# A decoder layer on one core: the key bias added by VectorE instead of a matmul, the normalisation of later groups on ScalarE

## The chip, the cores and the metric

The kernel runs on one core of a Trainium2 chip. The metric is the device time of one execution in microseconds. TensorE multiplies matrices, VectorE and ScalarE do elementwise work, GpSimd (POOL) does small side work, SyncE (SP) starts most transfers. Every engine takes its own instructions strictly in order and waits for the others by semaphores.

## The reference: what is computed

One pre-norm decoder layer over x of 2 x 2048 rows of 512 numbers, in float32. `ln` is a layer norm without weights. Only the first part matters here:

```
xn = ln(x)
k = xn @ Wk + bk ;  q = xn @ Wq + bq ;  v = xn @ Wv + bv
K = elu(k) + 1 ;    Q = elu(q) + 1                       # 8 heads of 64
KV = sum over rows of K v^T ; x1 = x + (Q KV) / (Q . sum of K)
x2 = x1 + cross attention of ln(x1) with a context of 77 rows
out = x2 + mixture of 8 experts, top 2, on ln(x2)
```

## The kernel before

The rows are worked on in 8 groups of 512 (4 tiles of 128 rows). Stage one goes over all groups and makes the keys' feature map, the queries' for the first four groups, and the Gram matrix xn^T K from which KV follows. Stage two goes over the groups again (attention, cross attention, routing), stage three over the experts. The change touches stage one alone.

Float32 accuracy comes from splitting each operand into a high and a low part (`_hi` by ScalarE, `_lo` = value - high by VectorE), and each product is three matmuls of 512 columns (`three`, lines 915 to 919). So a group s (0 to 7) of stage one is, engine by engine:

- TensorE: `project(s)`: four key tiles j = 0 to 3, each a bias product (L1023: a matrix of ones times the bias) and 12 products, into PSUM bank `pj[j % 2]`; in groups 0 to 3 four query tiles of 12 products (L917 to L919) more, into the same two banks. Then `gram(s)`, four tiles of 12 products into `pg`, and between them `turn(s + 1)`, 16 transposes (L935) of the next group's `xn` in two halves. The first half wants `xn`, the second also `xT_lo` of the first (s_tlo). In group 1 the cross attention's products (L951 to L975) stand between the query tiles, in group 2 L983 and L992.
- ScalarE: `turned_hi` (L688), `xn_hi` (L718, waits for the Gram products of the group before), then for each tile exp and relu of the bank (L695, L696: `job`), and for keys `k_hi` (L700).
- VectorE: `turned_lo`, `xn_lo` (both L1333), `next_stats(s + 1)` (L1337, L1343: mean and variance of the next input), then for each tile `kf` or `qT` from exp and relu (L1371: `job`), `k_lo` (L1333), and in the middle `normalise(s + 1)` (L1350: `xn`).
- POOL: the reciprocal of the standard deviation (L499, L500: `rstd_in`) and the sum of the keys (L548).

TensorE has two banks, so tile j waits until bank j - 2 has been read: `s_feat`, which ScalarE raises behind its relu. The order within an engine is written by hand.

Of the kernel before, what the change touches and what calls it, by code (L numbers as in the profile page):

```python
# [13 lines left out]
F32R = mybir.dt.float32r  # L14
# [21 lines left out]
BR = 33  # L36
# [42 lines left out]
def decoder(nc, x, wq, wk, wv, bq, bk, bv, ctxT, xwqT, xbq, xwk, xbk, xwv4, xbv4, wout, bout,  # L79
# [181 lines left out]
    with ExitStack() as ctx:  # L261
# [16 lines left out]
        s_bk = sem("bk_rows_cleared")  # L278
# [91 lines left out]
        XATTN_LOADS, WOUT_LOADS, WK_LOADS, WQ_LOADS, WV_LOADS = 7, 5, 3, 2, 2  # L370
# [118 lines left out]
        def _(pool):  # L489
# [180 lines left out]
        def _(act):  # L670
# [19 lines left out]
            def job(s, j):  # L690
                act.wait_ge(s_proj, FIRST[s] + j + 1)
                if s or j >= 2:
                    act.wait_ge(s_fm, FIRST[s] + j - 1)
                bias = 0.0 if j < TI else bq_c[:, j - TI:j - TI + 1]
                a.activation(fe[j % 2][:], pj[j % 2][:], ACT.Exp, bias=bias)  # L695
                a.activation(frl[j % 2][:], pj[j % 2][:], ACT.Relu, bias=bias).then_inc(s_feat, 1)  # L696
# [14 lines left out]
            for s in range(GROUPS):  # L711
# [202 lines left out]
        def _(pe):  # L914
# [855 lines left out]
```

## Time and profile before

| | |
|---|---|
| median of 3 runs | 1554.58 us (1553.37 to 1557.08) |
| the profiled execution | 1555.67 us, its span 1554.0 us |
| mean granted TensorE clock | 0.969 |
| TensorE busy | 1447.5 us (93%) |
| VectorE, ScalarE, POOL busy | 626.7, 569.1, 358.3 us |
| stage one | 0 to 292.2 us |

The span is from the first to the last instruction; the time of the execution has 1.67 us more around it. Busy time is the time in which an engine had an instruction in hand. DVE, ACT, POOL, PE stand for VectorE, ScalarE, GpSimd, TensorE; PEld is the load of a matmul's weights.

### The profile page before, as it was taken

Reading aid. Unit: us, or ns where it says so; the run is one execution under the profiler, and the core shown is the slowest. Engines: PE = TensorE matmul, PEld = TensorE weight load, DVE = VectorE, ACT = ScalarE, POOL = GpSimd, SP = SyncE. Lnnn points to the kernel's source line nnn. Section 1 sums busy time; section 2 is a strip of 40 time slices with the busy share of each in tenths; the row PEclk is TensorE's granted clock in tenths of the full one; section 3 lists DMA queues with packets and bytes.
Section 4 is the critical chain, followed back from the end, with each engine's and each line's share of the span. In section 5 each row is a group of like instructions: output and inputs, shape, how many; then the busy total and the mean of one; then the engine's idle time right before and its main releaser. Section 6 shows DMA issues by size and latency. Waiting matters only on the chain.

```text
span 1554.0 us, 20925 instructions
## 1 busy us (share of the span) xinstructions
PE 1447.5 (93%) x7326; PEld 1215.5 (78%) x7327; DVE 626.7 (40%) x1383; ACT 569.1 (37%) x977; POOL 358.3 (23%) x346
## 2 busy tenths in 40 slices
PE   6999999999984499999999899999999999999998
PEld 4867877787872387888888788898789888897886
DVE  5634565467876143411342531215431431215211
ACT  4433433257865133312342522224432432214211
POOL 3201232137665302011112112021112112021111
PEclk9999999999996599999999999999999999999999
DMA  9200221229546416121353332035533342035112
GB/s 197 52 4 28 82 82 54 82 79 210 129 124 196 135 56 163 55 40 14 64 178 54 120 99 40 0 54 176 155 88 54 103 114 40 0 54 149 13 40 27
DMA packets 78985, 132.19 MB, mean 85 GB/s; under 512 B 30388, under 2 KB 30516, under 8 KB 77912
## 3 DMA queue, kind: packets, MB, share of 16 engines
q1 hardware_dynamic: 62520, 97.40, 22.0%
q0 software_dynamic: 16416, 34.16, 11.8%
q8 instruction: 28, 0.46, 0.1%
q14 instruction: 21, 0.17, 0.0%
HBM read 93.63 MB, written 37.91 MB: 85 GB/s over the span
## 4 chain that ended last, share of the span: by engine, by line
PE 81%; DVE 5%; POOL 4%; DMA 4%; issue 3%; ACT 2%; SPq 0%; ACTq 0%; DVEq 0%; POOLq 0%
PE pg L917 16%; PE pg L918 15%; PE pg L919 15%; PE pj L917 8%; PE pj L919 8%; PE pj L918 8%; POOL slot_table L589 2%; DMA slot_table<-pack,dest 2%; PE pt L1270 1%; PE pg L1176 1%; PE pj L1148 1%; DVE w_lo L1333 1%; DMA stage<-w 1%; PE pg L1114 1%; PE pt L935 1%
## 5 line engine op out<-in xcount | busy, mean ns | idle before, releaser
L917 PE MATMUL pg<-xe_hi,w_hi 128*128 128x512 f32 (+2 forms) x1088 | 394.0, 362 | 22.2 <-DVE w_lo L1333 12.8
L918 PE MATMUL pg<-xe_lo,w_hi 128*128 128x512 f32 (+2 forms) x1088 | 393.0, 361 | 0.0
L919 PE MATMUL pg<-xe_hi,w_lo 128*128 128x512 f32 (+2 forms) x1088 | 392.7, 361 | 0.0
L1705 DVE TENSOR_TENSOR hp<-gl,pg 128x512 f32<-128x512 f32 (+1 forms) x136 | 87.1, 641 | 606.7 <-ACT gl L870 606.7
L650 POOL DMA_INDIRECT out_rows<-ost,etab x62 | 99.2, 1600 | 801.2 <-ACT ost L897 402.5
L917 PEld LDWEIGHTS pg<-xe_hi,w_hi 128*128 128x128 f32 x1088 | 207.6, 191 | 53.9 <-DVE w_lo L1333 14.8
L870 ACT ACTIVATE gl<-pg 128x512 f32<-128x512 f32 (+1 forms) x136 | 76.1, 560 | 456.6 <-PE pg L919 456.6
L919 PEld LDWEIGHTS pg<-xe_hi,w_lo 128*128 128x128 f32 x1088 | 207.7, 191 | 28.4
L918 PEld LDWEIGHTS pg<-xe_lo,w_hi 128*128 128x128 f32 x1088 | 207.7, 191 | 28.2
L917 PE MATMUL pj<-w_hi,hg_hi 128*128 128x512 f32 x464 | 183.3, 395 | 0.0
L919 PE MATMUL pj<-w_hi,hg_lo 128*128 128x512 f32 x464 | 180.8, 390 | 0.0
L918 PE MATMUL pj<-w_lo,hg_hi 128*128 128x512 f32 x464 | 180.7, 390 | 0.0
L1333 DVE TENSOR_TENSOR w_lo<-stage,w_hi 128x1024 fp32r<-128x1024 f32 x96 | 115.0, 1223 | 33.5 <-ACT w_hi L810 32.8
L897 ACT ACTIVATE ost<-pj,etab 128x512 f32<-128x512 f32 x62 | 42.6, 688 | 200.6 <-PE pj L919 194.3
L810 ACT ACTIVATE w_hi<-stage 128x1024 fp32r<-128x1024 f32 x96 | 99.0, 1057 | 40.3 <-DMA stage<-w 39.3
L919 PEld LDWEIGHTS pj<-w_hi,hg_lo 128*128 128x128 f32 x464 | 87.1, 188 | 18.3
L918 PEld LDWEIGHTS pj<-w_lo,hg_hi 128*128 128x128 f32 x464 | 87.2, 188 | 17.2
L917 PEld LDWEIGHTS pj<-w_hi,hg_hi 128*128 128x128 f32 x464 | 87.2, 188 | 17.1
L1333 DVE TENSOR_TENSOR hg_lo<-hp,hg_hi 128x512 fp32r<-128x512 f32 (+1 forms) x136 | 87.0, 639 | 1.9
L873 ACT ACTIVATE hg_hi<-hp 128x512 fp32r<-128x512 f32 (+1 forms) x136 | 79.8, 587 | 4.1 <-DVE hp L1705 4.1
L589 POOL DMA_INDIRECT slot_table<-pack,dest x64 | 67.5, 1055 | 23.1 <-issue 17.2
L1333 DVE TENSOR_TENSOR xe_lo<-pt,xe_hi 128x512 fp32r<-128x512 f32 x66 | 42.6, 685 | 71.3 <-ACT xe_hi L850 71.1
(233 smaller groups left out, 1946.3 us busy)
## 6 DMA issues: line engine op xcount, KB each, us to landing
stage<-w SPq DMA_DIRECT2D x96, 512.0 KB, 4.9
xr<-x SPq DMA_DIRECT2D x8, 1024.0 KB, 9.4
out_rows<-xr SPq DMA_DIRECT2D x8, 1024.0 KB, 7.2
x_rows<-xn SPq DMA_DIRECT2D x8, 1024.0 KB
x_in<-x SPq DMA_DIRECT2D x7, 1024.0 KB, 5.5
late_xT<-xT_hi SPq DMA_DIRECT2D x2, 1024.0 KB, 3.9
late_xT<-xT_lo SPq DMA_DIRECT2D x2, 1024.0 KB, 6.0
xT_hi<-late_xT SPq DMA_DIRECT2D x2, 1024.0 KB, 4.7
```

The costliest lines, as they stand in the source:

```text
L589: p.indirect_dma_start(out=table, out_offset=bass.IndirectOffsetOnAxis(ap=dest[:, c:c + 1], axis=0), in_=pack[:, c, :], in_offset=None).th ...
L650: p.indirect_dma_start(out=out, out_offset=bass.IndirectOffsetOnAxis(ap=etab[:, t, 0:1], axis=0), in_=ost[i % 2][:], in_offset=None, compu ...
L810: a.activation(w_dst(s), stage[s % STG][:], ACT.Copy).then_inc(s_w_hi, 1)
L870: a.activation(gl[j % 2][:, 0:w], pg[:, j % 2, 0:w], ACT.Gelu).then_inc(s_gl, 1)
L873: a.activation(hg_hi[:, j - 1, 0:w], hp[(j - 1) % 2][:, 0:w], ACT.Copy).then_inc(s_hghi, 1)
L897: a.activation(ost[i % 2][:], pj[i % 2][:], ACT.Copy, scale=etab[:, t, 1:2].bitcast(F32)).then_inc(s_yev, 1)
L917: nc.tensor.matmul(o, lh, rh, start=start, stop=False)
L918: nc.tensor.matmul(o, lh, rl, start=False, stop=False)
L919: return nc.tensor.matmul(o, ll, rh, start=False, stop=stop)
L935: ins = nc.tensor.transpose(pt[k % 2][:, i * P:(i + 1) * P], xn[:, i, k * P:(k + 1) * P], ident[:])
L1333: return v.tensor_tensor(dst, src, hi.bitcast(F32), ALU.subtract)
L1705: v.tensor_tensor(hp[j % 2][:, 0:w], gl[j % 2][:, 0:w], pg[:, 2 + j % 2, 0:w], ALU.mult).then_inc(s_hp, 1)
```

## The change

The bias product of each key tile goes (32 products), with the ones, the bias parts and their making. Instead the bias is loaded into all 128 partitions (`bk_all`), and VectorE adds it to each key tile out of PSUM into a tile `kb[j % 2]` (`key_bias`); ScalarE's exp and relu then read `kb`. The bank is free for TensorE when the addition is done (`s_kb`). VectorE's order in a tile becomes: bias of tile j, `k_lo` of tile j - 1, `kf` of tile j. ScalarE makes `k_hi` of tile j - 1 ahead of exp and relu of tile j, no longer behind. The normalisation of groups 1 to 7 goes from VectorE to ScalarE, as x * rstd + shift, at the same place of the loop; POOL makes the shift with two small instructions more.

```diff
@@ SyncE
-            for dst, src in ((wk_raw[:], wk.rearrange("(k p) n -> p k n", p=P)),
-                             (bk_rows[0:1, :], bk), (bk_rows[BR - 1:BR, :], bk)):
-                sp.dma_start(dst, src).then_inc(s_wk_in, 16)
+            sp.dma_start(wk_raw[:], wk.rearrange("(k p) n -> p k n", p=P)).then_inc(s_wk_in, 16)
+            sp.dma_start(bk_all[:], bk.broadcast_to([P, D])).then_inc(s_bk, 16)
@@ GpSimd, rstd_in
-                inverse_std(0).then_inc(s_rstd, 1)
+                if s == 0:
+                    inverse_std(0).then_inc(s_rstd, 1)
+                    return
+                pool.wait_ge(s_xn, s)
+                p.tensor_scalar(neg_mean[0][:], mv[0][:, :, 0], -1.0, None, ALU.mult)
+                step(inverse_std(0))
+                p.tensor_tensor(shift[0][:], neg_mean[0][:], rstd[0][:], ALU.mult).then_inc(s_rstd, 1)
@@ ScalarE
-            a.activation(ones_r[:], ones[:], ACT.Copy).then_inc(s_yev, 1)
-            a.activation(bk_parts[:], zrow[:], ACT.Copy).then_inc(s_bk, 1)
             act.wait_ge(s_wk_in, 16 * WK_LOADS)
             a.activation(wk_hi[:], wk_raw[:], ACT.Copy).then_inc(s_whi, 1)
-            act.wait_ge(s_bk, 1)
-            a.activation(bk_parts[0:1, :], bk_rows[0:1, :], ACT.Copy)
-            a.activation(bk_parts[BR - 1:BR, :], bk_rows[BR - 1:BR, :], ACT.Copy).then_inc(s_whi, 1)
...
+            def normalise(s):
+                act.wait_ge(s_rstd, s + 1)
+                act.wait_ge(s_xnhi, s)
+                act.wait_ge(s_xnlo, s)
+                for i in range(TI):
+                    ins = a.activation(xn[:, i, :], x_in[:, i, :], ACT.Identity, bias=shift[0][:, i:i + 1],
+                                       scale=rstd[0][:, i:i + 1])
+                ins.then_inc(s_xn, 1)
@@ ScalarE, loop over a group's tiles
+                    if 1 <= j <= TI:
+                        khi(s, j - 1)
                     if j < JOBS[s]:
                         job(s, j)
-                    if 1 <= j <= TI:
-                        khi(s, j - 1)
+                    if s + 1 < GROUPS and j == (TI if s == 0 else 2):
+                        normalise(s + 1)
@@ TensorE, project
-                    if s or j >= 2:
-                        pe.wait_ge(s_feat, FIRST[s] + j - 1)
+                    if j >= 2 or s:
+                        b, c = (s, j - 2) if j >= 2 else (s - 1, JOBS[s - 1] + j - 2)
+                        if c < TI:
+                            pe.wait_ge(s_kb, b * TI + c + 1)
+                        else:
+                            pe.wait_ge(s_feat, FIRST[b] + c + 1)
...
-                        mm(o, ones_r[:], bk_parts[:], start=True, stop=False)
@@ VectorE
+            def key_bias(s, j):
+                dve.wait_ge(s_proj, FIRST[s] + j + 1)
+                if s or j >= 2:
+                    b, c = (s, j - 2) if j >= 2 else (s - 1, TI + j - 2)
+                    dve.wait_ge(s_feat, FIRST[b] + c + 1)
+                v.tensor_tensor(kb[j % 2][:], pj[j % 2][:], bk_all[:], ALU.add).then_inc(s_kb, 1)
@@ VectorE, loop over a group's tiles
-                    if j < JOBS[s]:
-                        job(s, j)
+                    if j < TI:
+                        key_bias(s, j)
                     if 1 <= j <= TI:
                         ...
+                    if j < JOBS[s]:
+                        job(s, j)
                     if s == 0 and j == 2:
                         next_stats(1)
-                    if s + 1 < GROUPS and j == (TI if s == 0 else 2):
-                        normalise(s + 1)
```

The first place is VectorE at the start of group 1 (it reads alike in groups 2 to 6), from `xn_lo` on. In the kernel before, with `exp_relu_ready` for s_feat and `proj_psum_ready` for a finished bank:

```order
L1333 TENSOR_TENSOR xn_lo<-xn,xn_hi 128x2048 [waits xn_hi_ready]
L1337 BN_STATS st_71<-x_in 128x6 [waits x_in_loaded]
L1337 BN_STATS st_71<-x_in 128x6 x3
L1343 BN_AGGR mv_73<-st_71 128x2 [waits dve_step]
L1343 BN_AGGR mv_73<-st_71 128x2 x3
L1371 SCALAR_TENSOR_TENSOR kf_142<-fe_138,frl_140 128x512 [waits k_lo_ready,k_sum_added,exp_relu_ready]
L1371 SCALAR_TENSOR_TENSOR kf_143<-fe_139,frl_141 128x512 [waits k_lo_ready,k_sum_added,exp_relu_ready]
L1333 TENSOR_TENSOR k_lo<-kf_142,k_hi 128x512 [waits feature_map_ready,k_hi_ready]
L1371 SCALAR_TENSOR_TENSOR kf_142<-fe_138,frl_140 128x512 [waits k_lo_ready,k_sum_added,exp_relu_ready]
L1333 TENSOR_TENSOR k_lo<-kf_143,k_hi 128x512 [waits feature_map_ready,k_hi_ready]
```

In the changed kernel:

```order
L1353 TENSOR_TENSOR xn_lo<-xn,xn_hi 128x2048 [waits xn_hi_ready]
L1357 BN_STATS st_71<-x_in 128x6 [waits rstd_ready,x_in_loaded]
L1357 BN_STATS st_71<-x_in 128x6 x3
L1363 BN_AGGR mv_73<-st_71 128x2 [waits dve_step]
L1363 BN_AGGR mv_73<-st_71 128x2 x3
L1381 TENSOR_TENSOR kb_155<-pj,bk_all 128x512 [waits exp_relu_ready,proj_psum_ready]
L1400 SCALAR_TENSOR_TENSOR kf_142<-fe_138,frl_140 128x512 [waits k_lo_ready,k_sum_added,exp_relu_ready]
L1381 TENSOR_TENSOR kb_156<-pj,bk_all 128x512 [waits exp_relu_ready,proj_psum_ready]
L1353 TENSOR_TENSOR k_lo<-kf_142,k_hi 128x512 [waits feature_map_ready,k_hi_ready]
L1400 SCALAR_TENSOR_TENSOR kf_143<-fe_139,frl_141 128x512 [waits k_lo_ready,k_sum_added,exp_relu_ready]
L1381 TENSOR_TENSOR kb_155<-pj,bk_all 128x512 [waits exp_relu_ready,proj_psum_ready]
```

The addition of tile 0 stands behind `xn_lo` and the eight statistics instructions, where the first `kf` stood.

The second place is ScalarE in the same group, between the tiles 1 and 4. Before (`k_hi` of tile 0 is the first row):

```order
L700 ACTIVATE k_hi<-kf_142 128x512 [waits feature_map_ready]
L695 ACTIVATE fe_138<-pj 128x512 [waits feature_map_ready,proj_psum_ready]
L696 ACTIVATE frl_140<-pj 128x512
L700 ACTIVATE k_hi<-kf_143 128x512 [waits feature_map_ready]
L695 ACTIVATE fe_139<-pj 128x512 [waits feature_map_ready,proj_psum_ready]
L696 ACTIVATE frl_141<-pj 128x512
L700 ACTIVATE k_hi<-kf_142 128x512 [waits feature_map_ready]
L695 ACTIVATE fe_138<-pj,bq_c 128x512 [waits feature_map_ready,proj_psum_ready]
L696 ACTIVATE frl_140<-pj,bq_c 128x512
L700 ACTIVATE k_hi<-kf_143 128x512 [waits feature_map_ready]
```

In the changed kernel (`fe` and `frl` are exp and relu; the first row is relu of tile 1):

```order
L700 ACTIVATE frl_141<-kb_156 128x512
L714 ACTIVATE k_hi<-kf_143 128x512 [waits feature_map_ready]
L697 ACTIVATE fe_138<-kb_155 128x512 [waits feature_map_ready,k_with_bias_ready]
L700 ACTIVATE frl_140<-kb_155 128x512
L708 ACTIVATE xn<-x_in,shift_81,rstd_77 128x512 [waits xn_lo_ready,xn_hi_ready,rstd_ready]
L708 ACTIVATE xn<-x_in,shift_81,rstd_77 128x512 x3
L714 ACTIVATE k_hi<-kf_142 128x512 [waits feature_map_ready]
L697 ACTIVATE fe_139<-kb_156 128x512 [waits feature_map_ready,k_with_bias_ready]
L700 ACTIVATE frl_141<-kb_156 128x512
L714 ACTIVATE k_hi<-kf_143 128x512 [waits feature_map_ready]
L697 ACTIVATE fe_138<-pj,bq_c 128x512 [waits feature_map_ready,proj_psum_ready]
```

Four normalisations now stand between relu of tile 2 and `k_hi` of tile 2.

The third place is the start of ScalarE's program. Before:

```order
L674 ACT_TABLE_LOAD
L674 ACTIVATE ones_r<-ones 128x128 [waits consts_ready]
L675 ACTIVATE bk_parts<-zrow 128x512
L677 ACTIVATE wk_hi<-wk_raw 128x2048 [waits wk_loaded]
L679 ACTIVATE bk_parts<-bk_rows 1x512 [waits bk_rows_cleared]
L680 ACTIVATE bk_parts<-bk_rows 1x512
L688 ACTIVATE xT_hi<-pt 128x512 [waits xT_psum_ready] x4
```

In the changed kernel:

```order
L679 ACT_TABLE_LOAD [waits wk_loaded]
L679 ACTIVATE wk_hi<-wk_raw 128x2048 [waits consts_ready]
L687 ACTIVATE xT_hi<-pt 128x512 [waits xT_psum_ready] x4
L732 ACTIVATE xn_hi<-xn 128x2048 [waits xn_ready]
L735 ACTIVATE wq_hi<-wq_raw 128x2048 [waits wq_loaded]
L697 ACTIVATE fe_138<-kb_155 128x512 [waits k_with_bias_ready]
```

The load of the function table now stands behind the wait for the key weights.

## Rows read from the trace of the kernel before

**Rows 1.** The page: busy time and instructions by engine.
```profile
PE 1447.5 (93%) x7326; PEld 1215.5 (78%) x7327; DVE 626.7 (40%) x1383; ACT 569.1 (37%) x977; POOL 358.3 (23%) x346
```

**Rows 2.** Window of group 6, from its first key product to group 7's.
```profile
core 0: us, PE busy (x) PEld busy (x) DVE busy (x) ACT busy (x) POOL busy (x), PEclk, DMA share, GB/s
243.35:269.45 26.10, 24.78 (x117) 20.32 (x116) 17.43 (x25) 10.63 (x17) 8.21 (x6) 1.00 0.13 41
```

**Rows 3.** Waits of TensorE in 0:330 us: for whom, us, times, longest.
```profile
PE pt L935 <- DVE xn L1350: 13.8, 3, 11.2
PE pt L992 <- DVE vpT L1432: 2.7, 1, 2.7
```

**Rows 4.** Timeline of TensorE, group 6: start, length, what it does.
```profile
243.35 0.39 PE L1023 MATMUL pj<-bk_parts,ones_r 128*128 128x512 f32 x1
...
255.14 0.39 PE L917 MATMUL pg<-k_hi,xn_hi 128*128 128x512 f32 x1
...
259.33 1.09 PE L935 MATMUL pt<-ident,xn 128*128 128x128 f32 x8 [1.32 <-DVE xn L1350]
...
263.04 1.07 PE L935 MATMUL pt<-ident,xn 128*128 128x128 f32 x8
```

**Rows 5.** Timeline of VectorE, group 6.
```profile
245.56 2.29 DVE L1333 TENSOR_TENSOR xn_lo<-xn,xn_hi 128x2048 fp32r<-128x2048 f32 x1 [6.07 <-ACT xn_hi L718]
247.77 2.47 DVE L1337 BATCH_NORM_STATS2 st<-x_in 128x6 f32<-128x512 f32 x4
...
250.56 1.26 DVE L1371 SCALAR_TENSOR_TENSOR kf<-fe,frl 128x512 f32<-128x512 f32 x2
...
254.69 1.78 DVE L1333 TENSOR_TENSOR k_lo<-kf,k_hi 128x512 fp32r<-128x512 f32 x1
256.40 2.88 DVE L1350 TENSOR_SCALAR xn<-x_in,mv,rstd 128x512 f32<-128x512 f32 x4
```

**Rows 6.** Timeline of ScalarE, group 6.
```profile
243.61 1.92 ACT L718 ACTIVATE xn_hi<-xn 128x2048 fp32r<-128x2048 f32 x1 [4.95 <-PE pg L919]
246.50 0.60 ACT L695 ACTIVATE fe<-pj 128x512 f32<-128x512 f32 x1 [0.97 <-PE pj L919]
246.99 0.59 ACT L696 ACTIVATE frl<-pj 128x512 f32<-128x512 f32 x1
```

**Rows 7.** Lines of VectorE and ScalarE, shapes apart, 0:290 us.
```profile
L1333 DVE TENSOR_TENSOR xT_lo<-pt,xT_hi 128x512 fp32r<-128x512 f32 x32 | 20.7, 685 | 23.3 <-ACT xT_hi L688 23.1
L700 ACT ACTIVATE k_hi<-kf 128x512 fp32r<-128x512 f32 x32 | 20.2, 632 | 13.8 <-DVE kf L1371 13.8
...
L695 ACT ACTIVATE fe<-pj,bq_c 128x512 f32<-128x512 f32 x16 | 11.0, 690 | 39.7 <-PE pj L919 39.7
```

**Rows 8.** Timeline of ScalarE in stage two: four normalisations, pipelined.
```profile
348.79 2.93 ACT L794 ACTIVATE xn<-xr,shift,rstd 128x512 f32<-128x512 f32 x4
```

**Rows 9.** Timeline of the start, all engines.
```profile
0.86 1.28 ACT L674 ACT_TABLE_LOAD   x1 [0.71 <-PEq L1760]
...
2.26 0.31 ACT L674 ACTIVATE ones_r<-ones 128x128 fp32r<-128x128 f32 x1
...
10.03 1.91 ACT L677 ACTIVATE wk_hi<-wk_raw 128x2048 fp32r<-128x2048 f32 x1 [6.94 <-DMA bk_rows<-bk]
...
15.01 1.29 DVE L1333 TENSOR_TENSOR xT_lo<-pt,xT_hi 128x512 fp32r<-128x512 f32 x2
...
22.54 2.28 DVE L1333 TENSOR_TENSOR wq_lo<-wq_raw,wq_hi 128x2048 fp32r<-128x2048 f32 x1
```

**Rows 10.** Timeline of TensorE, group 0: first and second key tile, first Gram product.
```profile
19.14 0.80 PE L1023 MATMUL pj<-bk_parts,ones_r 128*128 128x512 f32 x1 [1.41 <-DVE xT_lo L1333]
...
24.86 0.57 PE L1023 MATMUL pj<-bk_parts,ones_r 128*128 128x512 f32 x1
...
44.80 0.39 PE L917 MATMUL pg<-k_hi,xn_hi 128*128 128x512 f32 x1
```

**Rows 11.** Window of low clock behind TensorE's wait at L992.
```profile
128.00:131.20 3.20, 3.20 (x9) 2.47 (x9) 0.00 (x0) 0.25 (x1) 0.00 (x0) 0.53 0.00 0
```

More of the change, by code:

```diff
@@ L35 @@
 CK, XH = 77, 32
-BR = 33
 PADW = 96
@@ L193, in decoder @@
     wv_sb = fr("wv_sb", [P, KC, D])
-    ones_r = fr("ones_r", [P, P], F32R)
-    bk_parts = fr("bk_parts", [P, D], F32R)
-    bk_rows = fr("bk_rows", [BR, D])
+    bk_all = fr("bk_all", [P, D])
+    kb = [fr(f"kb{i}", [P, D]) for i in range(2)]
     bv_row = fr("bv_row", [1, D])
@@ L277, in decoder @@
         s_dself = sem("dve_meta_step")
-        s_bk = sem("bk_rows_cleared")
+        s_bk = sem("bk_loaded")
+        s_kb = sem("k_with_bias_ready")
         s_whi = sem("front_w_hi")
@@ L369, in decoder @@
         table_t = table[0:TRASH, :].rearrange("(t p) w -> p t w", p=P)
-        XATTN_LOADS, WOUT_LOADS, WK_LOADS, WQ_LOADS, WV_LOADS = 7, 5, 3, 2, 2
+        XATTN_LOADS, WOUT_LOADS, WK_LOADS, WQ_LOADS, WV_LOADS = 7, 5, 1, 2, 2
         block = ctx.enter_context(nc.Block())
@@ L690, in job @@
             def job(s, j):
-                act.wait_ge(s_proj, FIRST[s] + j + 1)
+                if j < TI:
+                    act.wait_ge(s_kb, s * TI + j + 1)
+                else:
+                    act.wait_ge(s_proj, FIRST[s] + j + 1)
                 if s or j >= 2:
                     act.wait_ge(s_fm, FIRST[s] + j - 1)
-                bias = 0.0 if j < TI else bq_c[:, j - TI:j - TI + 1]
-                a.activation(fe[j % 2][:], pj[j % 2][:], ACT.Exp, bias=bias)
-                a.activation(frl[j % 2][:], pj[j % 2][:], ACT.Relu, bias=bias).then_inc(s_feat, 1)
+                from_, bias = (kb[j % 2], 0.0) if j < TI else (pj[j % 2], bq_c[:, j - TI:j - TI + 1])
+                ins = a.activation(fe[j % 2][:], from_[:], ACT.Exp, bias=bias)
+                if s == 0 and j == 0:
+                    ins.then_inc(s_yev, 1)
+                a.activation(frl[j % 2][:], from_[:], ACT.Relu, bias=bias).then_inc(s_feat, 1)
+            def normalise(s):
[6 more added lines that the diff above has]
+                ins.then_inc(s_xn, 1)
             def khi(s, i):
@@ L1001, in project @@
                     if s == 0 and j == 0:
+                        pe.wait_ge(s_whi, 1)
+                        pe.wait_ge(s_wlo, 1)
+                    if s == 0 and j == TI:
                         pe.wait_ge(s_whi, 2)
                         pe.wait_ge(s_wlo, 2)
-                    if s == 0 and j == TI:
-                        pe.wait_ge(s_whi, 3)
-                        pe.wait_ge(s_wlo, 3)
                     if s == 1 and j == TI:
@@ L1016, in project @@
                         value_logits()
-                    if s or j >= 2:
-                        pe.wait_ge(s_feat, FIRST[s] + j - 1)
+                    if j >= 2 or s:
+                        b, c = (s, j - 2) if j >= 2 else (s - 1, JOBS[s - 1] + j - 2)
+                        if c < TI:
+                            pe.wait_ge(s_kb, b * TI + c + 1)
+                        else:
+                            pe.wait_ge(s_feat, FIRST[b] + c + 1)
                     o = pj[j % 2][:]
@@ L1022, in project @@
                         tk = slice(j * P, (j + 1) * P)
-                        mm(o, ones_r[:], bk_parts[:], start=True, stop=False)
                         for k in range(KC):
                             ins = three(o, x_hi[:, k, tk], x_lo[:, k, tk], wk_hi[:, k, :], wk_lo[:, k, :],
-                                        False, k == KC - 1)
+                                        k == 0, k == KC - 1)
                         ins.then_inc(s_proj, 1)
@@ L1344, in aggregate, with normalise_first @@
                 ins.then_inc(done, 1)
-            def normalise(s):
-                dve.wait_ge(s_rstd, s + 1)
+            def normalise_first():
+                dve.wait_ge(s_rstd, 1)
                 for i in range(TI):
@@ L1445, in next_stats @@
                 dve.wait_ge(s_xin, 16 * s)
+                dve.wait_ge(s_rstd, s)
                 link(stats(x_in, 0, range(TI)))
@@ L1453, in _ @@
             aggregate(0, s_stat)
-            normalise(0)
+            normalise_first()
             dve.wait_ge(s_whi, 1)
             low(wk_lo[:], wk_raw[:], wk_hi[:]).then_inc(s_wlo, 1)
-            dve.wait_ge(s_whi, 2)
-            low(bk_parts[BR - 1:BR, :], bk_rows[BR - 1:BR, :], bk_parts[BR - 1:BR, :]).then_inc(s_wlo, 1)
+            dve.wait_ge(s_bk, 16)
             for s in range(GROUPS):
@@ L1466, in _ @@
                 if s == 0:
-                    dve.wait_ge(s_whi, 3)
+                    dve.wait_ge(s_whi, 2)
                     low(wq_lo[:], wq_raw[:], wq_hi[:]).then_inc(s_wlo, 1)
@@ L1480, in _ @@
                         value_logits_out()
-                    if j < JOBS[s]:
-                        job(s, j)
+                    if j < TI:
+                        key_bias(s, j)
                     if 1 <= j <= TI:
```

## The prediction

> **What bounds the kernel now.** I read the page first: TensorE is busy for 93% of the span, VectorE and ScalarE for 40% and 37% [rows 1]. That is a mean over three stages, so I cut stage one into its groups. In group 6 TensorE is busy for 24.78 of 26.10 us, VectorE for 17.43, ScalarE for 10.63 [rows 2]. The list of waits says what the rest is: in 330 us TensorE waited three times for `xn`, 13.8 us in all and 11.2 of it at the start, and once 2.7 us for `vpT` [rows 3]. So stage one goes at TensorE's pace, and what is taken from TensorE is won, if nobody is late in its place. Whether somebody is late can't be seen in busy shares, since the two small engines have time to spare. It has to be read from the order in which VectorE works through a group, so the timelines of group 6 are the main view [rows 4 to 6]. I count t from the group's first key product, at 243.35.
>
> **What is removed.** 52 products stand between 243.35 and 255.14 [rows 4], 0.227 us each. Group 0 begins slowly: its first 13 products take 5.72 us, 0.44 each [rows 10]. The 32 bias products are so 31 x 0.227 + 0.44 = **7.5 us** of TensorE's time.
>
> **The first two key tiles.** Before, a bank was read by ScalarE: exp of tile 0 starts at t = 3.15, relu ends at 4.23 [rows 6], long before TensorE wants the bank for tile 2. Now VectorE must read it, and it is VectorE that is away then. `xn_lo` waits for `xn_hi`, which ends at t = 2.18 [rows 6], as it begins only when the last Gram product has read the old one; `xn_lo` stands at 2.21, the statistics at 4.42, and the first `kf` follows at 7.21 [rows 5]. The addition takes the place of that `kf`, by the order shown above. Its price: no row adds the bias, but `xT_lo` is the same kind, 128 x 512 from PSUM and SBUF into SBUF, 0.685 us [rows 7]. The bounds are 0.61, the distance of two such in the stream (1.29 for two, 0.68 for the last) [rows 9], and 0.7. So bank 0 is free at t = 7.9, and 7.95 with the 0.05 that a semaphore takes here (`xn_hi` ends at 245.53, `xn_lo` starts at 245.56). TensorE has finished tiles 0 and 1 after 24 products, at 5.44, and waits **2.5 us**. This comes in groups 1 to 6, where the statistics stand ahead: 6 x 2.5 = **15.1 us**. In group 7 there are none: VectorE is free at 2.21 + 2.2 = 4.4, adds until 5.1, and nothing waits. Nothing hides the wait, for TensorE's next instruction is the one that waits.
>
> **The loop behind it.** From there the tiles go hand in hand. If an addition starts at a, it ends at a + 0.69; exp and relu take 1.08 from PSUM [rows 6], and about 1.15 from SBUF (`k_hi` reads SBUF in 0.632 [rows 7], exp reads PSUM in 0.60 [rows 6]), so they end at a + 1.9; `kf` ends at a + 2.6, and the next addition may start about then, at a + 2.6. TensorE's tile takes 2.72. So the loop keeps up, but never makes good. Additions start at 7.2, 9.8, 12.4; keys are done on TensorE at 7.95 + 5.44 = 13.4 (before: 11.8 [rows 4]).
>
> **The moved normalisation.** It leaves VectorE (2.88 us, stretched [rows 5]) and stands on ScalarE behind relu of tile 2, which ends at 14.3. Its price is 2.93 for four [rows 8], same function, shape, scale and bias tile. POOL's two more instructions are hidden: it gets the statistics at 7.2 and is wanted at 14.2. So `xn` is ready at 17.2. Queued behind it on ScalarE are `k_hi` of tile 2 (to 17.75), exp and relu of tile 3 (to 18.85), then on VectorE `kf` of tile 3 (to 19.6), and `k_hi` again (to 20.3). Before, that last `kf` began when `xn` ended, at 259.28, t = 15.9 [rows 5]. Now it is 18.9, 3.0 later. Who waits for that:
>
> - Groups 5 and 6 (keys only): the Gram tile ends at 16.1, the transposes want `xn` at 17.2, wait 1.1. They and the next Gram tile take 3.71 (259.33 to 263.04 [rows 4]), to 20.9. The second half wants `xT_lo`: `xT_hi` ends at 20.8, `k_lo` of tile 3 and `xT_lo` on VectorE at 21.7, wait 0.85. Before, the wait was 255.14 + 2.72 = 257.86 to 259.33, 1.47. `k_lo` can be held up as well: beside POOL's sum it took 1.78 in place of 0.69 [rows 5], 1.1 more. I take half of that, 0.55: (1.1 + 1.4 - 1.47) x 2 = **2.0 us**; bounds 1.0 and 3.2. In group 4 the products for KV stand ahead of this place and cover it.
> - Group 3: the first query tile's exp and relu come behind that `k_hi`, 0.69 + 0.58 = 1.27 [rows 7], to 21.45. TensorE has done two query tiles at 18.85 and waits 2.65 for the bank.
> - Group 2: TensorE waits for `vpT`, which VectorE copies behind that `kf`. It is 3.0 later, TensorE 2.5 - 0.9 = 1.6 later, so the wait of 2.7 [rows 3] grows by 1.4.
> - Group 1: the products for the scores wait likewise for what VectorE makes behind `kf`. There was no wait before and some slack; between 0 and 1.4 I take 1.0.
> - Group 0: no statistics ahead, but `wq_lo` until 24.82 [rows 9], so additions at 24.9, 27.5, 30.1. Statistics of the next group (2.8) stand between `kf` of tile 2 and the addition of tile 3, which ends at 36.1. TensorE's first tile ends at 24.4 [rows 10], and it is through with the first query tile at 35.5: waits 0.6 for that bank. Exp and relu of the first query come behind `kf` and `k_hi` of tile 3, to 39.9: wait 1.05. The normalisation follows, to 42.75, and exp and relu of the second query end at 44.0: wait 1.4. In all 3.1; the Gram products start at 46.8 in place of 44.80 [rows 10].
>
> These four groups together: 2.65 + 1.4 + 1.0 + 3.1 = **8.15 us**, bounds 3 (if the handovers are faster than my loop) and 9.
>
> **The start.** Here I expected a gain, since `wk_hi` no longer waits for two small bias loads and a `_lo` of 0.7 us goes. But the table load, 1.28 us at 0.86 [rows 9] in the shade of the loads, now stands behind the wait for the key weights. They have landed at some time up to 10.0; `wk_hi` started at 10.03 and will start 1.28 + 0.1 behind their landing. If that is 8, `xT_lo` starts 1.4 earlier than at 15.01, if it is 10.0, 0.6 later. I take **0**. The table load's price by the row is 1.28, and `ones_r` starts 0.12 behind its end. The Trainium skill (ScalarE: Activation LUTs, What ACT_TABLE_LOAD costs) adds a drain of about 1.38 us to 1.28; no row here shows it, and with it the sum would be 1.4 higher.
>
> **Sum.** -7.5 + 15.1 + 2.0 + 8.15 + 0 = +17.8 us. The profiled execution of before took 1555.67, of which its span is 1554.0; 1.1 above the median. On the median 1554.58 it gives **1572.3 us**, 1.1% slower. Stages two and three are as they were and only start later.
>
> **Rivals.**
> 1. Only the first wait costs; the rest of the loop has more slack than I gave it. For it: busy shares of 40%. Against: the last `kf` of before waited for nothing but its own engine's `xn`. -7.5 + 15.1 = +7.6, 1562.2. Chance 0.2.
> 2. The clock falls too. Behind the wait for `vpT` the granted clock was 0.53 for 3.2 us [rows 11], that is the lower level, 1.2 GHz, and cost 0.47 x 3.2 = 1.5 us of work. Six new waits are nearly as long. But in groups 2, 3, 5, 6 a slower stretch only shortens the later wait, so I gave it nothing. With four more stretches that are not hidden, +6, 1578.3. Chance 0.15.
> 3. Faster. If VectorE is done with the statistics sooner, TensorE does not wait and the 7.5 us are won: 1547.1. It decides at 0.91 us of wait for each group (four products): the addition of tile 0 must end before t = 6.3, so `xn_lo` and the statistics would have to take 1.6 of their 5.0 us less. Nothing in the change shortens them. Chance 0.04.
> 4. GpSimd holds VectorE up at every turn. `k_lo` at 1.78 [rows 5] is such a case; held in full each time behind the last tile, the late groups cost 3.2 in place of 2.0, 1573.5. The Trainium skill (SBUF — State Buffer, Who interferes with whom) says that a VectorE instruction with two SBUF inputs is blocked for the whole of a GpSimd instruction that reads SBUF, and one with a single SBUF input is not. By that the addition is free of it. This is inside the forecast's range.
> 5. The changes cancel or do nothing: about 1554.6, up to 3 us more. Half of the first wait and all that follows would have to be absent. Chance 0.06, half of it within 0.2% and half above.
>
> The forecast, 1566 to 1576 with rival 4, has 0.55. A measurement of this kernel tells some 0.2%, 3.1 us, from no change. Faster 0.04, within 0.03, slower 0.93. The range takes in rival 1 and rival 2 with their bounds: 1561.5 to 1580.
>
> **What would show it.** In the list of waits: TensorE at the first product of a key tile, six times about 2.5 us, for `kb` of VectorE; at query tiles for relu, 1 to 2.7 us; at `xn`, now of ScalarE, about 1.1 in groups 5 and 6. No bias products; TensorE's busy time some 7 us less in a longer span. Group 6 takes 28.7 us from first key product to first key product in place of 26.10, group 3 some 4.2 us more than before (1.6 and 2.65). The first key product stays near 19.1. The forecast is wrong if VectorE's addition of tile 0 starts before t = 6.3, or if the tiles run ahead of my 2.6 us.

## The result and the profile after

The changed kernel takes 1580.36 us in the median (1576.76 to 1585.87) beside 1555.64 us (1553.37 to 1557.08) for the kernel before on the same chip. The ratio is 1.0147, interval 1.0113 to 1.0182: it is slower, by 22.9 us on 1555.64. The forecast was 1572.3 us, range 1561.5 to 1580.0. On its own basis, 1554.58 us, the ratio gives 1577.4 us: the sign and the first wait were right, the size 5 us too small, and two terms of the sum were off in opposite directions (told in "Why the prediction was right"). The median itself lies 0.4 us above the top of the range.

The profiled execution took 1579.12 us, its span 1577.4, the mean clock 0.963. The busy times on the page, to be read beside [rows 1]:

```profile
PE 1450.9 (92%) x7294; PEld 1214.2 (77%) x7295; DVE 629.4 (40%) x1386; ACT 588.5 (37%) x1001; POOL 352.9 (22%) x360
```

32 matmuls are gone, and still TensorE is busy 3.4 us longer, where the forecast had some 7 us less: part of the work ran at the lower clock. The waits of TensorE in 0:340 us, beside [rows 3] (`frl` is relu):

```profile
PE pj L933 <- DVE kb L1381: 14.7, 7, 2.5
PE pt L951 <- DVE xn L1370: 11.5, 1, 11.5
PE pt L951 <- DVE xT_lo L1353: 4.3, 3, 3.0
PE pt L1008 <- DVE vpT L1461: 3.0, 1, 3.0
...
PE pj L933 <- ACT frl L700: 2.4, 3, 0.9
...
PE pt L951 <- ACT xn L708: 0.6, 1, 0.6
```

The first row is new: seven waits for the addition, six of 2.3 to 2.5 us (groups 1 to 6) and one of 0.63 in group 0. The timeline of TensorE shows one, in group 1, whose first key product stands at 59.87:

```profile
65.08 0.39 PE L935 MATMUL pj<-wk_hi,xT_lo 128*128 128x512 f32 x1
67.79 0.50 PE L933 MATMUL pj<-wk_hi,xT_hi 128*128 128x512 f32 x1 [2.32 <-DVE kb L1381]
```

In the stream a product starts 0.23 us behind the one before it. From 65.08 + 0.23 to 67.79 are 2.48 us; the other five waits, counted so, are 2.48 or 2.49 and, in group 4, 2.67. And the timeline of VectorE says what the addition was behind:

```profile
62.08 2.29 DVE L1353 TENSOR_TENSOR xn_lo<-xn,xn_hi 128x2048 fp32r<-128x2048 f32 x1 [5.98 <-ACT xn_hi L732]
64.28 2.46 DVE L1357 BATCH_NORM_STATS2 st<-x_in 128x6 f32<-128x512 f32 x4
66.78 0.38 DVE L1363 BATCH_NORM_AGGREGATE mv<-st 128x2 f32<-128x6 f32 x4
67.08 0.66 DVE L1381 TENSOR_TENSOR kb<-pj,bk_all 128x512 f32<-128x512 f32 x1
68.96 0.69 DVE L1400 SCALAR_TENSOR_TENSOR kf<-fe,frl 128x512 f32<-128x512 f32 x1 [1.22 <-ACT frl L700]
69.56 0.68 DVE L1381 TENSOR_TENSOR kb<-pj,bk_all 128x512 f32<-128x512 f32 x1
70.34 1.22 DVE L1353 TENSOR_TENSOR k_lo<-kf,k_hi 128x512 fp32r<-128x512 f32 x1
...
72.30 0.69 DVE L1381 TENSOR_TENSOR kb<-pj,bk_all 128x512 f32<-128x512 f32 x1
...
78.60 0.69 DVE L1400 SCALAR_TENSOR_TENSOR kf<-fe,frl 128x512 f32<-128x512 f32 x1 [0.35 <-ACT frl L700]
```

67.08 is t = 7.21, where [rows 5] has the first `kf`. The last `kf` starts at t = 18.73.

The lengths from first key product to first key product, read from TensorE's timelines, in us; the row of group 7 runs from its first product to stage two's first (`pg<-kv,qT`), and the row of stage one from the start of the span to that product:

| | before | after | change | forecast |
|---|---|---|---|---|
| start (first key product) | 19.14 | 19.83 | +0.69 | 0 |
| group 0 | 38.36 | 40.04 | +1.68 | +2.0 |
| group 1 | 49.87 | 53.14 | +3.27 | +2.6 |
| group 2 | 41.71 | 43.73 | +2.02 | +3.0 |
| group 3 | 36.37 | 40.67 | +4.30 | +4.25 |
| group 4 | 31.80 | 35.23 | +3.43 | +1.6 |
| groups 5, 6, each | 26.10 | 28.40 | +2.30 | +2.6 |
| group 7 and the sums | 24.30 | 23.39 | -0.91 | -0.9 |
| stage one | 293.75 | 312.83 | +19.1 | +17.75 |
| stages two and three | 1260.25 | 1264.57 | +4.3 | 0 |

The window of group 6, beside [rows 2], in the same columns:

```profile
261.04:289.44 28.40, 25.84 (x114) 20.65 (x113) 17.04 (x25) 13.74 (x21) 7.42 (x8) 0.94 0.12 38
```

The group's four bias products are gone, and yet TensorE is busy for 1.06 us more than before: the granted clock was 0.94. The list of waits doesn't show this. In group 6 it cost nothing, as told below; in groups 1 and 4 it is a part of the loss. Five windows over stage one have PEclk at 1.00, 0.97, 0.92, 0.96, 0.98 (they are shown beside e10).

### The profile page after: what moved, and what is told of

The parts are those of the page before. It is cut to its first block, busy times and chain, and to the rows that moved or that the text cites. A ratio compares the mean times of both kernels' runs of the same rounds, so it can differ in the third digit from the quotient of the medians.

```text
span 1577.4 us, 20954 instructions
## 1 busy us (share of the span) xinstructions
PE 1450.9 (92%) x7294; PEld 1214.2 (77%) x7295; DVE 629.4 (40%) x1386; ACT 588.5 (37%) x1001; POOL 352.9 (22%) x360
## 4 chain that ended last, share of the span: by engine, by line
PE 76%; ACT 5%; DMA 5%; DVE 5%; issue 4%; POOL 4%; SPq 0%; ACTq 0%; POOLq 0%; DVEq 0%
PE pg L933 15%; PE pg L935 15%; PE pg L934 15%; PE pj L933 8%; PE pj L935 7%; PE pj L934 7%; POOL slot_table L593 2%; DMA stage<-w 2%; DMA slot_table<-pack,dest 2%; PE pt L1290 1%; PE pg L1196 1%; DVE st L1357 1%; DVE w_lo L1353 1%; PE pj L1168 1%; PE pt L951 1%
## 5 line engine op out<-in xcount | busy, mean ns | idle before, releaser
L933 PE MATMUL pg<-xe_hi,w_hi 128*128 128x512 f32 (+2 forms) x1088 | 393.9, 362 | 22.2 <-issue 13.2
```

Source lines behind the costliest of these rows:

```text
L933: nc.tensor.matmul(o, lh, rh, start=start, stop=False)
```

## The experiments

The theory on trial (A): TensorE waits because the addition of tile 0 stands behind `xn_lo` and the statistics; the moved normalisation makes the rest of the loop late. The rivals (B): the normalisation itself does the harm; the addition as such is too slow; the clock does.

Whole times scatter by more than most of these edits are worth, so the profile of stage one is read beside them. For all kernels, in us; the last column counts the stretches of some 3.4 us at the lower clock in between:

| | first key product | stage two's first product | between | low clock |
|---|---|---|---|---|
| before | 19.14 | 293.75 | 274.61 | 1 |
| changed | 19.83 | 312.83 | 293.00 | 5 |
| e1 | 20.17 | 296.25 | 276.08 | 2 |
| e2 | 20.49 | 294.84 | 274.35 | 1 |
| e3 | 19.47 | 316.00 | 296.53 | 6 |
| e4 | 19.25 | 312.12 | 292.87 | 5 |
| e5 | 18.92 | 287.08 | 268.16 | 0 |
| e6 | 18.19 | 285.01 | 266.82 | 1 |
| e7 | 18.05 | 280.79 | 262.74 | 1 |
| e8 | 19.58 | 285.31 | 265.73 | 0 |
| e9 | 18.94 | 279.06 | 260.12 | 0 |
| e10 | 19.15 | 297.36 | 278.21 | 0 |

The first key product moves with the landing of the key weights, which scatters: ScalarE's first instruction that waits for them starts between 9.78 and 11.38 us. What an edit does to the groups is therefore read from the third column. The kernel before measured 1557.85 us beside e1 to e4, 1557.22 beside e5 to e8 and 1557.44 beside e9 and e10; the ratios are to those runs.

**e1: the statistics ahead of the wait for `xn_hi`.** While VectorE waits for `xn_hi` (5.98 us in the row above) it has nothing to do; the statistics are put there, in front of `xn_lo`.

```diff
@@ VectorE, group s
+                if s >= 1 and s + 1 < GROUPS:
+                    next_stats(s + 1)
                 dve.wait_ge(s_xnhi, s + 1)
...
-                if s >= 1 and s + 1 < GROUPS:
-                    next_stats(s + 1)
```

> The changed kernel with the statistics of the next group moved ahead of the wait for xn_hi, into the time in which VectorE waits for the last Gram product; the addition of tile 0 then stands behind xn_lo alone. Theory A (the addition of tile 0 is late because xn_lo and the statistics stand ahead of it on VectorE): the addition starts at t = 4.4 in place of 7.2, the six waits of 2.3 us at the third key product are gone, and the kernel is 14 to 20 us faster than the changed one, 1560 to 1566. Rival B (ScalarE's longer queue, with the normalisation, sets the pace of the group whatever VectorE does first): the wait moves to another place of the group and less than 5 us are won. Rival C (the lower clock behind the waits is most of the loss): the group lengths fall by more than the waits that vanish.

1557.39 us, ratio to before 1.0002 (0.9965 to 1.004). One order, nothing left out, takes back the loss, to within that interval and beyond the 1560 that was expected. The addition of tile 0 starts at t = 4.42. The waits of TensorE in 0:296 us:

```profile
...
PE pt L951 <- DVE xT_lo L1353: 4.8, 3, 2.7
PE pj L933 <- ACT frl L700: 3.5, 3, 1.8
PE pt L1008 <- DVE vpT L1461: 2.9, 1, 2.9
...
PE pj L933 <- DVE kb L1381: 1.0, 2, 0.6
PE pt L951 <- ACT xn L708: 0.9, 2, 0.5
```

The six long waits for `kb` are gone, but for one of 0.33 in group 4. The others, for relu (group 3: 1.83, 0.71 in the changed kernel), `vpT` and `xn`, stayed, and they eat what the bias products gave: from the first key product to stage two it is 1.5 us longer than before.

This also weighs the clock. Groups 1 to 6 became 17.4 us shorter, and the waits for `kb` in them 14.6. What is beyond the waits stands mainly in groups 1 and 4, whose stretches of low clock are gone: 3.93 us less in group 1 for a wait of 2.48, 3.68 in group 4 for 2.18. So the clock has some 3 us of the loss, and the waits the most.

**e2: the normalisation alone** on the kernel before; the bias product stays.

```diff
@@ ScalarE, loop over a group's tiles (before)
+                    if s + 1 < GROUPS and j == (TI if s == 0 else 2):
+                        normalise(s + 1)
@@ VectorE
-                    if s + 1 < GROUPS and j == (TI if s == 0 else 2):
-                        normalise(s + 1)
```

> The kernel before with the second part of the change alone: normalisation of groups 1 to 7 on ScalarE, bias product kept. Theory A: harmless or slightly good; the waits for xn in groups 5 and 6 (1.3 us each) go, the bank is still released by ScalarE; within -6 and +1 us of before, no wait at a key product. Rival B: the normalisation of 2.9 us in ScalarE's queue holds up exp and relu of the next tiles, TensorE waits for relu in every group, 3 us or more slower than before.

1556.91 us, ratio 0.9994 (0.9971 to 1.0017). Stage two starts at 294.84, 1.1 later, but only because the first key product is 1.35 later, at 20.49 (the weights landed late); between the two it is 0.3 us shorter than before. Group 0 is 1.7 longer (a wait of 1.42 for relu at a query tile), groups 5 and 6 are 0.7 shorter, group 2 too. The normalisation by itself does no harm that can be measured.

**e3: the bias alone**; the normalisation is back on VectorE.

```diff
@@ ScalarE (after)
-                    if s + 1 < GROUPS and j == (TI if s == 0 else 2):
-                        normalise(s + 1)
@@ VectorE
+                    if s + 1 < GROUPS and j == (TI if s == 0 else 2):
+                        normalise_dve(s + 1)
```

> The changed kernel with the normalisation back on VectorE: the bias part alone. Theory A: the six waits of 2.3 us at the third key product stay, since the normalisation is not ahead of them; VectorE has 2 to 3 us more in the middle of each group, so the later waits grow; 0 to 6 us slower than the changed kernel, 1580 to 1586. Rival B: without the normalisation on ScalarE most of the loss is gone, below 1572.

1581.47 us, ratio 1.0161 (1.0115 to 1.0207); by the medians it can't be told from the changed kernel. The waits of TensorE in 0:314 us:

```profile
PE pj L925 <- DVE kb L1373: 15.9, 8, 2.5
PE pt L943 <- DVE xn L1362: 12.6, 2, 11.3
PE pt L943 <- DVE xT_lo L1345: 5.4, 3, 2.9
PE pt L1000 <- DVE vpT L1453: 2.3, 1, 2.3
PE pj L925 <- ACT frl L694: 2.2, 2, 1.5
...
```

The six waits are there without the normalisation's move, and stage two starts at 316.0, 3.2 later than in the changed kernel; groups 5 and 6 are 0.92 and 1.24 longer. So the loss is the bias edit's, and beside it the move to ScalarE helps, as far as one profile of each shows. Rival B's first form falls. The second, that the addition as such is too slow, falls by e1, which keeps all 32 additions.

**e4: the function table loaded early.** One activation of four columns ahead of the wait for the key weights.

```diff
@@ ScalarE, start (after)
+            a.activation(ge[:], half_neg[:], ACT.Exp)
             act.wait_ge(s_wk_in, 16 * WK_LOADS)
```

> The changed kernel with one small exp ahead of the wait for the key weights, so that the function table is loaded in the shade of the loads. wk_hi starts 1.28 us earlier, and the first key product up to 1.3 us earlier than 19.83, if nothing else is late; the group lengths stay. 0.5 to 1.3 us faster than the changed kernel, below what the times can tell; the profile decides. If the table load costs more than its 1.28 us (a drain of about 1.4 us more), the first key product comes 2 us or more earlier.

1574.97 us, ratio 1.0109 (1.0072 to 1.0147). The timeline of ScalarE, changed kernel first, then e4:

```profile
10.27 1.28 ACT L679 ACT_TABLE_LOAD   x1 [10.11 <-DMA wk_raw<-wk]
11.56 1.91 ACT L679 ACTIVATE wk_hi<-wk_raw 128x2048 fp32r<-128x2048 f32 x1
```

```profile
0.86 1.28 ACT L678 ACT_TABLE_LOAD   x1 [0.71 <-PEq L1790]
2.26 0.20 ACT L678 ACTIVATE ge<-half_neg 128x4 f32<-128x4 f32 x1
10.97 1.91 ACT L680 ACTIVATE wk_hi<-wk_raw 128x2048 fp32r<-128x2048 f32 x1 [8.51 <-DMA wk_raw<-wk]
```

In the changed kernel the weights are there by 10.27 and `wk_hi` waits 1.28 us more for the table. In e4 they landed 0.7 later by chance, so I count from the first instruction behind their landing to the first key product: 19.83 - 10.27 = 9.56 us in the changed kernel, and 9.56 in e1 and e3 too; 19.25 - 10.97 = 8.28 in e4, and 8.27 in e5, e6, e7 and e9. The difference is 1.28 to 1.29, the load's length. Before, from 10.03 to 19.14, it was 9.11. The medians of e4 and of the changed kernel can't be told apart by so little.

The Trainium skill (ScalarE: Activation LUTs, What ACT_TABLE_LOAD costs) states a drain of about 1.38 us beside the load for a switch to another set. `wk_hi` begins 0.01 us behind the load's end, so nothing of it shows behind the load; ahead of it ScalarE had no work in hand, and what a drain would cost there this place can't show.

**e5, e6, e7: the other waits, one after the other**, each on top of the last. e5 is e1 with the early table, and in groups 1 to 3 the normalisation moves from key tile 2 to the second query tile (j = 5). In e6 group 0 has its normalisation and the next group's statistics one tile later. e7 lets TensorE make one Gram tile more ahead of the transposes in the groups without queries.

```diff
@@ ScalarE (e1 to e5, e6)
-                    if s + 1 < GROUPS and j == (TI if s == 0 else 2):
+                    if s + 1 < GROUPS and j == (NORM_0 if s == 0 else TI + 1 if s < EARLY else 2):
                         normalise(s + 1)
@@ VectorE; e5: NORM_0, STATS_0 = 4, 2; e6: 5, 3
-                    if s == 0 and j == 2:
+                    if s == 0 and j == STATS_0:
                         next_stats(1)
@@ TensorE (e7)
-                gram(s, range(1))
+                late_turn = 1 if s >= EARLY else 0
+                gram(s, range(1 + late_turn))
```

> The first experiment's kernel (statistics early) with the normalisation on ScalarE moved in groups 1 to 3 from key tile 2 to the second query tile, and the table loaded early. Theory A (in the groups with queries the waits of 1.8 to 2.9 us for relu and for vpT come from the normalisation queued ahead of k_hi, exp and relu of tile 3): the wait at group 3's query tile goes, the one for vpT in group 2 shrinks to 1 us or less, group 3 takes 37.4 us or less in place of 39.2; 3 to 5 us faster than the first experiment. Rival (the loop of VectorE and ScalarE itself is too slow for the query tiles): the waits stay within 0.5 us.

e5: 1553.88 us, ratio 0.9984 (0.9956 to 1.0013). Stage two starts at 287.08, 9.2 us earlier than in e1; group 3 went from 39.20 to 35.78 and its wait for relu is gone, the wait for `vpT` went from 2.87 to 1.04. Not all of the 9.2 is the moved normalisation: 1.25 is the earlier first key product, and the two stretches of low clock that e1 has, in groups 2 and 3, are gone too. In the medians it is 3.5 us; they scatter over 20 us here.

> The same, and in group 0 the statistics one tile later (behind kf of tile 3) and the normalisation one tile later. Theory A: the three waits of group 0 (0.63, 0.70, 0.95 us) go or shrink to under 0.5 in all, group 0 takes 38 to 39 us in place of 40.4; 1 to 2 us faster than the run before. Rival: they are due to the loop itself and stay.

e6: 1547.86 us, ratio 0.9933 (0.9909 to 0.9958). Group 0 went from 39.81 to 36.87, with no wait left in it, a little more than expected. Stage two starts only 2.1 us earlier than in e5, since a stretch of low clock is back in group 2; what else lies between the medians, 6.0 us apart, isn't in stage one.

> The same, and in groups 4 to 6 each half of the transposes one Gram tile later, so that xn and xT_lo are asked for later. The waits of 0.45 and 1.05 us in groups 5 and 6 go; each takes 24.1 us (24.2 of products and 1.7 of transposes with no wait would be 25.2 less what overlaps) to 25.3. With hardly a wait left the removed 7.3 us of products must show: 1546 to 1550, 6 to 10 us faster than before. If it stays within 3 us of before, the products were not worth their time and my sum is wrong in its first term.

e7: 1543.40 us, ratio 0.9915 (0.9892 to 0.9938), faster than both kernels and than the 1546 to 1550 expected. Groups 5 and 6 take 23.55 us, in place of 26.10 before and of the 24.1 expected at least: 96 products of 0.227 are 21.8, and the 16 transposes take the rest, 1.8. The waits of TensorE in 0:281 us that remain behind the start:

```profile
PE pt L1010 <- DVE vpT L1464: 1.0, 1, 1.0
PE pg L1137 <- DVE gT L1410: 0.5, 1, 0.5
PE pj L935 <- DVE kb L1384: 0.3, 1, 0.3
```

**e8: e7's order with the bias product**, so that the edit's own worth is seen. It adds no bias on VectorE; ScalarE reads and frees the banks and makes `k_hi` behind exp and relu, as before, and the start is the old one.

```diff
@@ TensorE (e7 to e8)
+                        mm(o, ones_r[:], bk_parts[:], start=True, stop=False)
@@ VectorE
-                    if j < TI:
-                        key_bias(s, j)
```

> The same order of everything as in the run before (statistics early, later normalisation in groups 0 to 3, later transposes in groups 4 to 6, ScalarE normalising), but with the bias product kept and no addition on VectorE. Theory A: the 32 products are worth their full 7.3 us when nobody is late, so this is 5.5 to 7.5 us slower than the run before, and 1 to 5 us faster than the kernel before. Rival (the addition makes VectorE and ScalarE late even in a good order, and eats the gain): within 2 us of the run before.

1550.12 us, ratio 0.9963 (0.9935 to 0.9992). Groups 5 and 6 take 24.46 and 24.45, so 0.91 more than in e7, four products; likewise group 1 (49.82 and 48.91). From the first key product to stage two it is 265.73 in place of 262.74: 3.0 of the 7.3 us that the products are worth, since in group 2 e7 has a wait and a stretch of low clock that e8 has not (39.15 and 37.33). Beside e9, which has no such stretch either, it is 5.6. So not all of the 7.3 us comes back even there. The medians of e8 and e7 are 6.7 apart, as expected, but 1.5 of that is e8's later start, and what remains isn't in stage one. Some half of what e7 wins over the kernel before comes from the order (the ratios say 5.8 of 13.2 us; in the profiles, from the first key product to stage two, 8.9 of 11.9), and needs no change of the bias.

**e9: `vpT` copied a tile earlier**, on e7.

```diff
@@ VectorE, group 2
-                    if s == 2 and j == TI:
-                        vp_turned_out()
...
+                    if s == 2 and j == TI - 1:
+                        vp_turned_out()
```

> The fastest version so far (all waits mended) with the copies of vpT on VectorE ahead of kf of key tile 3 in group 2, no longer behind. Theory A: the wait of 1.0 us for vpT goes; with it the low clock behind it if the wait caused that: group 2 takes 38.1 us if the clock still falls, 36.5 if not, in place of 39.15. 1 to 2.7 us faster, 1541 to 1543; clear of the kernel before by 0.7% or more. Rival (the clock falls through the many short products around that place, not through the wait): a stretch at the lower clock stays in group 2.

1543.55 us, ratio 0.9926 (0.9897 to 0.9955). In the profile group 2 goes from 39.15 to 36.92, the wait from 1.03 to 0.43, and the low clock behind it (0.56 in 122.0 to 125.4 of e7) is gone; the medians of e7 and e9 can't be told apart, where 1 to 2.7 us were expected.

**e10: the wait alone.** On the kernel before, TensorE waits ahead of its third key tile until the statistics are through. The bias product stays and nothing is moved.

```diff
@@ TensorE, project (before)
+                    if j == 2 and 1 <= s < GROUPS - 1:
+                        pe.wait_ge(s_stat, s + 2)
```

> The kernel before, with one wait added and nothing else: in groups 1 to 6 TensorE waits ahead of the third key tile for the statistics (t = 7.1 to 7.3, where the changed kernel's addition starts; the first two tiles with their bias products end at 5.9). By the first theory six waits of 1.2 to 1.5 us, and as ScalarE and VectorE follow TensorE only later in the group, most of it on the end: 5 to 9 us slower than before without low clock, and no new stretch of low clock, since the waits are under 1.5 us. By the rival that each wait costs more than itself through the clock: new stretches in most groups and 12 us or more. If TensorE's wait were harmless, within 2 us of before.

1560.72 us, ratio 1.0033 (1.0009 to 1.0058). The waits of TensorE in 0:300 us:

```profile
...
PE pj L1025 <- DVE mv L1345: 8.5, 6, 1.6
...
PE pt L992 <- DVE vpT L1434: 1.1, 1, 1.1
```

Six waits of 1.4 to 1.6 us, 8.5 in all, move stage two by 3.6 us only (297.36), less than the 5 to 9 expected; the medians say 3.3, the ratio 5.1. They are hidden in groups 5 and 6 (26.18 and 26.19 us), where the wait for `xn` is gone, and in group 2, where the wait for `vpT` shrank from 2.7 to 1.1 and the low clock behind it is gone. Groups 1, 3 and 4 are 1.63, 1.64 and 1.83 longer. The clock tells e10 from the changed kernel. Five windows of TensorE over stage one, the changed kernel first (busy time, granted clock, DMA share, GB/s), then e10:

```profile
25.00:68.00 43.00, 38.41 (x174) 1.00 0.71 35
68.00:128.00 60.00, 57.68 (x250) 0.97 0.05 18
128.00:172.00 44.00, 38.67 (x174) 0.92 0.07 25
172.00:214.00 42.00, 38.78 (x171) 0.96 0.20 75
214.00:290.00 76.00, 69.48 (x331) 0.98 0.20 70
```

```profile
25.00:68.00 43.00, 41.62 (x192) 1.00 0.78 33
68.00:128.00 60.00, 57.52 (x267) 1.00 0.09 25
128.00:172.00 44.00, 42.61 (x199) 1.00 0.11 39
172.00:214.00 42.00, 40.43 (x204) 1.00 0.21 76
214.00:290.00 76.00, 73.23 (x342) 1.00 0.23 86
```

With waits of 1.4 to 1.6 us the clock stayed at its upper level throughout. In the changed kernel, with 2.3 to 2.5, it fell five times: behind the wait for `kb` in groups 1, 3, 4 and 6, and in group 2 behind the wait of 3.01 for `vpT`, where it had fallen before the change too [rows 11]. The two kernels differ in more than these waits, so the pair alone doesn't show that the length decides. Nor are waits under 1.5 us always without a stretch, as the expectation has it: the 1.03 of e7 had one behind it.

## Why the prediction was right, and where it was off

**The first wait (15.1 us): right.** The addition starts at t = 7.21 as forecast, takes 0.66 to 0.69 (forecast 0.685), and TensorE stands still for 2.48 us, six times (2.67 in group 4): 15.1 us. e1 removes exactly this and the loss with it. e10 shows from the other side that a wait at this place is paid almost in full only in the groups that have no later wait to hide it in.

**The removed products (7.5 us): right.** Group 7, with no wait, is 0.91 shorter, four products of 0.227; e8 and e7 differ by 0.91 in groups 1, 5 and 6.

**The clock (rival 2): the step that failed.** I wrote "so I gave it nothing". The stretches came in groups 1, 2, 3, 4 and 6; the one in group 2 is the old one behind `vpT`, so four are new. The windows of TensorE over the first four, in groups 1 to 4 (busy time, granted clock):

```profile
69.30:72.70 3.40, 3.40 (x10) 0.54 0.00 0
134.00:137.40 3.40, 3.40 (x12) 0.52 0.16 57
164.90:168.30 3.40, 3.40 (x9) 0.54 0.00 0
205.90:209.30 3.40, 3.40 (x9) 0.55 0.00 0
```

Each costs some 0.46 x 3.4 = 1.6 us of work; it is the lower level, 1.2 GHz. I had argued that they are hidden in groups 2, 3, 5 and 6. It held in groups 3 and 6, and for group 2 e4 shows it: there the wait for `kb` was followed by a stretch, the wait for `vpT` shrank from 3.01 to 1.74, and the group is 0.4 longer only. In group 3 the wait for relu is 0.7 us in place of my 2.65, and the length is as forecast: the slower TensorE took what the wait would have taken. In group 6 the stretch is wholly hidden, 28.40 us like group 5 without one. But in groups 1 and 4 hardly anything stands behind. Group 4 is 1.8 longer than forecast. Group 1 takes 51.99 in e4, which has no stretch there but a later wait of 0.39, and 53.14 here. By my own reasoning groups 1 and 4 had no later wait, and I should have added two stretches, 3.2 us, and not treated it as a rival alone. Half of rival 2 was part of the forecast's own case; it measured 2.8 us (1.15 and 1.67).

**What stands behind the normalisation (2.0 and 8.15 us): too high in sum, and half right in name.** Without the clock, group 0 has waits of 0.63, 0.70 and 0.94 (forecast 0.6, 1.05, 1.4), group 1 gained 0.5 (1.0), group 2's wait for `vpT` grew by 0.3 (1.4), and groups 5 and 6 are 0.3 shorter than forecast. In all, what stands behind the first wait measures 8.0 us (the change of each group without the first wait and the clock, and with the products added back: 2.8, 0.55, 0.45 and 2.7 in groups 0 to 3, and 1.46 in groups 5 and 6 together) where the two terms have 10.15. That this 2.1 too much and the clock's 2.8 too little nearly cancel, so that stage one came out 1.3 us beside the forecast, is luck. The last `kf` stands at t = 18.73 (18.9): the loop was right, and TensorE came later than I had it (in group 5 it asks for `xn` at t = 16.4, not 16.1). But I put all this down to the move of the normalisation. e3 shows that keeping it on VectorE beside the additions is 3.5 us worse from the first key product to stage two, and e2 that the move alone makes that stretch 0.3 shorter. On the other hand e5 and e6 take the waits for relu and most of that for `vpT` away by moving the normalisation to a later tile (e6 with the statistics). So these waits want both: the tiles that the bias edit ties together, and a normalisation in their middle, on either engine.

**The start (0, bounds -1.4 and +0.6): +0.69.** The weights were there by 10.27, with the table load behind them; before, `wk_hi` started at 10.03. These 0.24 are chance (the starts scatter from 9.78 to 11.38). From there to the first key product it is 9.56 in place of 9.11, so the change itself costs 0.45: the load's 1.28 less some 0.83 for the making of the bias parts, which is gone.

**Stages two and three (0): +4.3 in the profile.** TensorE is busy 1176.6 us in them beside 1174.8. Stages two and three have the same code in the ten experiments, and took 1255.6 to 1266.4 us there. The changed kernel's 1264.6 lies in that scatter, and the one profile before has 1260.25. Whether the later start shifts them by a microsecond or two wasn't separated and stays open.

**The rivals.** "Only the first wait" falls, for the other waits are there. GpSimd at every turn (rival 4) has a real hold-up in it (told in the last section), but its sum fell: groups 5 and 6 lost 1.46 us behind the first wait, not 3.2. Faster and cancelled fall. But the condition that I gave for "faster", the addition ending before t = 6.3, can be met: e1 moves the statistics rather than shortening them (the addition ends at t = 5.1), and gets no gain from it until the later waits are mended too (e5 to e7).

## What to carry to other kernels

When a buffer's reader moves to another engine, look at what stands ahead of it in that engine's order, not at the engine's busy share: at 40% it still held up a TensorE at 93%. Fill the engine's existing idle time (here 5.98 us in front of `xn_lo`) with the work that isn't urgent, and mend the waits behind the first too, since each hides the next. And where a wait of some 2.5 us is added to a busy TensorE, reckon with a low-clock stretch behind it (here behind 13 of 18 such waits), and count it in every place with no later wait to hide it.

## What the hardware showed beside that

- **The clock and short waits.** Behind the 18 waits of 2.3 to 2.5 us for `kb` in the changed kernel, e3 and e4 came 13 stretches of some 3.4 us at the lower level (4, 5 and 4 of six each); behind the six of 1.4 to 1.6 us in e10 none. The length alone doesn't decide. In e6 and e7 the clock fell 2.3 us behind a wait of 1.03 for `vpT` (0.56 in the window of e7), in e5 it did not fall behind the same wait of 1.04, nor behind 1.09 in e10. What decides it stays open.
- **GpSimd and VectorE.** Two groups of lines by shape in the changed kernel, 0:312 us (count, busy, mean ns of one, idle before):

```profile
L1353 DVE TENSOR_TENSOR k_lo<-kf,k_hi 128x512 fp32r<-128x512 f32 x32 | 33.9, 1058 | 16.3 <-ACT k_hi L714 15.1
L1381 DVE TENSOR_TENSOR kb<-pj,bk_all 128x512 f32<-128x512 f32 x32 | 21.7, 679 | 1.7 <-PE pj L935 1.2
```

The same shape and nearly the same function (a subtraction, an addition), but `k_lo` has two inputs in SBUF and takes 1.06 us on average, up to 1.23; the addition has one in PSUM, and no one of its 32 took more than 0.69. GpSimd works beside both: 24 of the `k_lo` overlap one of its instructions and take 1.18 on average, the other 8 take 0.69. The Trainium skill (SBUF — State Buffer, Who interferes with whom) states that a VectorE instruction with two SBUF inputs contends with a GpSimd instruction that reads SBUF, and one with at most one SBUF input doesn't. The trace agrees. So rival 4's hold-up is real for `k_lo`, about 0.5 us, and was there before (1.04 on average, up to 1.78).
- **The table load** at the start of the changed kernel runs at 10.27, behind the wait for the weights, and at 0.86 as soon as an activation without that wait stands ahead. The move cost 1.3 us at the start and came from the removal of an instruction that had nothing to do with it. It isn't always so: in stage three of the same kernel a load runs at 554.73, and the activation behind it then waits 7.64 us for TensorE.
